# A two-layer attention kernel: ten groups' outputs sent by transfer and divided on GpSimd, and the sums sent ahead of the operands

## The reference

```python
# first block
xn = x * rsqrt(mean(x * x) + EPS) * rms_w
scale, shift = split(cond @ w_cond)
q, k, v = split((xn * (1 + scale) + shift) @ w_qkv)
q, k = rope(q), rope(k)
attn = softmax(einsum("bqhd,bkhd->bhqk", q, k) * DH ** -0.5)
x = einsum("bhqk,bkhd->bqhd", attn, v) @ w_out + x
# second block
xn = layer_norm(x, norm_w, norm_b)
q, k, v = xn @ q_w + q_b, xn @ k_w + k_b, (xn @ v_w + v_b) * mask
att = softmax(q k^T + (1 - mask) * -1e6)
y = att @ v
e = silu(cond) @ emb_w + emb_b
h = layer_norm(y, sb_norm_w, sb_norm_b) * (1 + scale_of(e)) + shift_of(e)
x = x + silu(h) @ out_w + out_b
```

## Time and profile before

| | us |
|---|---|
| median of 3 runs | 491.29 (490.81 to 492.58) |
| profiled execution | 491.88 |
| its span (first to last instruction) | 489.7 |
| PE busy | 478.3 (98%) |
| DVE busy | 385.4 (79%) |
| ACT busy | 342.3 (70%) |
| POOL busy | 313.6 (64%) |

### The profile page before, as it was taken

How to read it: one execution, slowest core, us unless ns; L and a number is a source line. 1 busy time by engine, 2 the same in 40 slices (tenths; PEclk the granted TensorE clock), 3 DMA queues, 4 the chain that set the end, 5 groups by cost and what they waited for, 6 DMA issues and landing times.

```text
span 489.7 us, 9703 instructions
## 1 busy us (share of the span) xinstructions
PE 478.3 (98%) x3197; PEld 179.7 (37%) x3197; DVE 385.4 (79%) x989; ACT 342.3 (70%) x677; POOL 313.6 (64%) x445
## 2 busy tenths in 40 slices
PE   7999899999999999999999999999999999999996
PEld 3553322322443325332443235334333323333234
DVE  3767896999886796859776698867899999999124
ACT  2662567898667785968667785776787788777853
POOL 5569976899885996789646792859990055005501
PEclk9999999999999999999999999999999999999999
DMA  7775156355322465225502361114311121111011
GB/s 255 200 199 190 48 170 228 112 154 157 117 66 68 126 172 152 62 80 139 151 13 69 110 182 46 46 39 116 108 46 44 45 88 45 44 46 45 1 44 44
DMA packets 41577, 49.79 MB, mean 102 GB/s; under 512 B 12388, under 2 KB 34036, under 8 KB 41272
## 3 DMA queue, kind: packets, MB, share of 16 engines
q1 hardware_dynamic: 33336, 31.84, 22.2%
q0 software_dynamic: 7904, 16.03, 11.3%
q10 hardware_dynamic: 288, 1.31, 0.8%
HBM read 27.62 MB, written 19.01 MB: 95 GB/s over the span
## 4 chain that ended last, share of the span: by engine, by line
PE 74%; DVE 12%; POOL 5%; issue 3%; DMA 2%; ACT 1%; SPq 0%; DVEq 0%; POOLq 0%; ACTq 0%
PE bank L596 18%; PE bank L642 11%; PE bank L570 10%; PE bank L579 10%; PE bank L558 9%; DVE masked L955 7%; PE bank L653 6%; PE bank L670 5%; DVE row_max L958 2%; PE bank L627 2%; POOL XN L930 1%; DMA sums<-oT 1%; PE bank L611 1%; ACT probs L780 1%; PE bank L604 1%
## 5 line engine op out<-in xcount | busy, mean ns | idle before, releaser
L780 ACT ACTIVATE probs<-bank 128x512 f32<-128x512 f32 x512 | 269.3, 600 | 71.7 <-PE bank L570 70.9
L958 DVE TENSOR_REDUCE row_max<-bank 128x1 f32<-128x512 f32 x256 | 159.4, 681 | 34.0 <-PE bank L579 33.7
L579 PE MATMUL bank<-k_s,q_s 64*128 64x512 f16 x512 | 178.7, 382 | 2.3 <-DVE row_max L958 1.2
L955 DVE CUSTOM_DVE_ANT_0 masked<-bank,mask_bias 128x512 bf16<-128x512 f32 x256 | 161.7, 686 | 19.2 <-PE bank L579 18.7
L558 PE MATMUL bank<-q_s,k_s 64*128 64x512 f16 x512 | 151.4, 380 | 0.3
L570 PE MATMUL bank<-shift,kx 64*128 64x512 f16 x512 | 148.7, 376 | 0.4 <-DMA shift<-shift_rows 0.4
L596 PE MATMUL bank<-probs,v_aug 128*17 128x512 f32 x1024 | 135.5, 598 | 0.7 <-ACT probs L780 0.7
L579 PEld LDWEIGHTS bank<-k_s,q_s 64*128 64x128 f16 x512 | 46.2, 93 | 157.1 <-DVE row_max L958 70.9
L642 PE MATMUL bank<-xT,wqkv 128*128 128x512 f32 x128 | 59.6, 606 | 1.0 <-DVE xT L1096 0.6
L570 PEld LDWEIGHTS bank<-shift,kx 64*128 64x128 f16 x512 | 46.8, 95 | 34.1 <-DMA shift<-shift_rows 0.9
L1236 POOL TENSOR_SCALAR scaled<-row_max 128x16 f32<-128x16 f32 x30 | 7.7, 255 | 79.9 <-DVE row_max L955 44.5
(11 more groups left out here) (123 smaller groups left out, 478.9 us busy)
## 6 DMA issues: line engine op xcount, KB each, us to landing
q_s<-q_parts SPq DMA_DIRECT2D x32, 256.0 KB, 3.2
k_s<-k_parts SPq DMA_DIRECT2D x32, 256.0 KB, 4.1
k_parts<-parts POOLq DMA_DIRECT2D x62, 128.0 KB, 3.1
q_parts<-parts POOLq DMA_DIRECT2D x60, 128.0 KB, 3.0
X<-in_x SPq DMA_DIRECT2D x4, 512.0 KB, 7.3
O<-oT SPq DMA_DIRECT2D x64, 32.0 KB, 2.0
roped<-inverses SPq DMA_DIRECT2D x16, 128.0 KB
y<-X SPq DMA_DIRECT2D x7, 256.0 KB, 2.2
```

The costliest lines, as they stand in the source:

```text
L579: nc.tensor.matmul(bank, m.q_s[slot][rows, i, queries], m.k_s[slot][rows, i, :], start=True, stop=True).then_inc(q.d_made, 1)
L780: act.activation(m.probs[k][:, h, :], bank, ACT.Exp, scale=1.0 if s >= B * NG else float(DH) ** -0.5)\
L955: dve.tensor_tensor_reduce(m.masked[D["max", n, k, h] % ND][:, :], bank, m.mask_bias[:, b, :], 1.0, LOWEST, ALU.add, ALU.max, to)\
L958: dve.tensor_reduce(to, bank, AX.X, ALU.max).then_inc(q.d_done, 1)
```

## The change

Groups 16 to 25 (`SENT` = 26) leave `turn_output` and `write_output` and go the first layer's way: sums, inverses and output rows by transfer. Their sums are inverted on Pool, as a power with exponent -1 on 128 partitions by 16 columns, and Pool divides the chunk in place. Then PE turns the chunk back (`turn_back`, four transposes for two groups) and ACT copies it to `tokens`, which lies where a weight was. Groups 26 to 31 stay with the transposes. Turns, `y` and statistics of the second layer move to other steps, Pool's list is written anew, and SP sends the sums ahead of the operands; the tile for the sums is doubled.

```diff
+SENT = LAYER + NG * (B - 2) + NG // 2
...
-PIECES[20] = ((), qk(1, LAST, 2, 3), (), v(1, LAST))
-PIECES[22] = (*one(turn("f1", 0)), (), ())
-PIECES[23] = ((), (), y(1, 0)[:1], ())
-PIECES[24] = ((), (), (), y(1, 0)[1:])
-PIECES[26] = (*one(turn("f1", 1)), (), ())
-PIECES[27] = ((), (), y(1, 1)[:1], ())
-PIECES[28] = ((), (), (), y(1, 1)[1:])
+PIECES[20] = ((), qk(1, LAST, 2, 3) + (("back", 0, 0),), (), ())
+PIECES[21] = ((), (), (("back", 0, 1),), v(1, LAST))
+PIECES[23] = (*one(turn("f1", 0)), (), (("back", 1, 0),))
+PIECES[24] = ((), (), y(1, 0)[:1], ())
+PIECES[25] = ((), (), (("back", 1, 1),), y(1, 0)[1:])
+PIECES[27] = (*one(turn("f1", 1)), (), (("back", 2, 0),))
+PIECES[28] = ((), (), y(1, 1)[:1], y(1, 1)[1:])
...
-for _b in range(B - 1):
-    STATISTICS[20 + NG * _b, 3] = ("f1", _b)
+for _b, _s in enumerate((21, 25, 28)):
+    STATISTICS[_s, 3] = ("f1", _b)
...
-        if op == "output" and k == 2 and s > LAYER:
+        if op == "output" and k == 2 and s > SENT:
             yield op, s - 1
-        if op == "output" and k == 3 and 0 < s <= LAYER:
+        if op == "output" and k == 3 and 0 < s <= SENT:
             yield "sums", s - 1
...
+        m.tokens = [m.wc[:, 2 * i:2 * i + 2, :].rearrange("p k n -> p (k n)").rearrange("p (t c) -> p t c", c=C)
+                    for i in range(2)]
...
-        m.sums = sb("sums", [P, KT * G])
+        m.sums = [sb(f"sums{i}", [P, KT * G]) for i in range(2)]
...
+    def turn_back(piece):
+        _, b, c = piece
+        bank = a_free(A[piece])
+        pe.wait_ge(q.divided, normalised(B + b, c))
+        for t in range(TPB):
+            last = nc.tensor.transpose(bank[:, t * P:(t + 1) * P], m.raw[b % 2][:, c, t * P:(t + 1) * P], m.ident[:, :])
+        last.then_inc(q.a_made, 1)
...
-        if s > LAYER:
+        if s > SENT:
             act.wait_ge(q.d_made, D["output", s - 1] + 1)
         elif s:
             act.wait_ge(q.output_out, group_out(s - 1))
...
+    def back(piece):
+        _, b, c = piece
+        bank = made(A[piece])
+        if b >= 2:
+            act.wait_ge(q.xn_made, TPB * NORMAL.index(("f1", b - 2)))
+        act.activation(m.tokens[b % 2][:, :, c * P:(c + 1) * P], bank.rearrange("p (t n) -> p t n", n=P), ACT.Copy)\
+            .then_inc(q.a_done, 1)
...
-        if op == "sums":
+        if op == "sums" and at[0] < LAYER:
             invert(*at)
...
-    def divide(b, c):
-        use = USES.index(("f0", b))
-        pool.wait_ge(q.output_out, group_out(NG * b + 2 * c + 1))
-        pool.wait_ge(q.inv_in[c], 32 * (b + 1))
-        await_read(pool, q, use - 2)
-        pool.tensor_tensor(m.xT[use % 2][:, c, :], m.raw[b % 2][:, c, :], m.inverse[c][:, :], ALU.mult)\
-            .then_inc(q.divided, 1)
+    def divide(pu, c):
+        layer, b = divmod(pu, B)
+        pool.wait_ge(q.output_out, group_out(NG * pu + 2 * c + 1))
+        pool.wait_ge(q.inv_in[c], 32 * (pu + 1))
+        to = raw = m.raw[b % 2][:, c, :]
+        if layer == 0:
+            use = USES.index(("f0", b))
+            await_read(pool, q, use - 2)
+            to = m.xT[use % 2][:, c, :]
+        pool.tensor_tensor(to, raw, m.inverse[c][:, :], ALU.mult).then_inc(q.divided, 1)
+    def invert(s):
+        pool.wait_ge(q.sums_in, 16 * (s + 1))
+        pool.wait_ge(q.inv_out, 16 * s)
+        pool.tensor_tensor(m.inv_sum[:, :, :, :].rearrange("p t h w -> p (t h w)"), m.sums[s % 2][:, :], m.minus_one[:, :],
+                           ALU.pow).then_inc(q.inv_made, 1)
...
-    for b in range(LAST):
-        negate(NG * (B + b) + 6)
-        rstd("f1", b)
-        normal("f1", b)
-        if b == 0:
-            add_bias(LAST, 0)
-        negate(NG * (B + b) + 7)
-        if b == 0:
-            add_bias(LAST, 1)
+    def silu(b):
         for h in range(CT):
             i, h = silu_ready(pool, q, ("turn", "f1", b, h))
             pool.tensor_scalar(m.tanh[h], m.tanh[h], 1.0, None, ALU.add).then_inc(q.tanh_step, 1)
             pool.wait_ge(q.tanh_step, CT * b + h + 1)
             pool.tensor_tensor(m.xT[i][:, h, :], m.tanh[h], m.halved[h], ALU.mult).then_inc(q.silu_made, 1)
-        for n in (NG * (B + b) + 8, NG * (B + b) + 9):
-            if n in POOL_SHIFTS:
-                negate(n)
+    pool.wait_ge(q.one_made, 1)
+    invert(16)
+    invert(17)
+    normalise(LAST)
+    divide(B, 0)
+    add_output_bias(LAST)
+    add_bias(LAST - 1, 0)
+    invert(18)
+    add_bias(LAST - 1, 1)
+    negate(21)
+    split(B + LAST, 0)
+    split(B + LAST, 1)
+    invert(19)
+    negate(22)
+    divide(B, 1)
+    invert(20)
+    split(B + LAST, 2)
+    split(B + LAST, 3)
+    negate(23)
+    rstd("f1", 0)
+    normal("f1", 0)
+    invert(21)
+    negate(24)
+    divide(B + 1, 0)
+    silu(0)
+    negate(25)
+    invert(22)
+    invert(23)
+    add_bias(LAST, 0)
+    negate(26)
+    divide(B + 1, 1)
+    invert(24)
+    add_bias(LAST, 1)
+    negate(27)
+    rstd("f1", 1)
+    normal("f1", 1)
+    invert(25)
+    negate(28)
+    divide(B + 2, 0)
+    silu(1)
+    negate(29)
+    negate(GROUPS - 2)
+    rstd("f1", 2)
+    normal("f1", 2)
+    negate(GROUPS - 1)
+    silu(2)
...
-        if s:
-            sp.wait_ge(q.inv_made, s)
-        sp.dma_start(m.sums[:, :], m.oT[DH::W32, :].rearrange("h (c n) -> h c n", n=KT * G)).then_inc(q.sums_in, 16)
+        if s >= 2:
+            sp.wait_ge(q.inv_made, s - 1)
+        sp.dma_start(m.sums[s % 2][:, :], m.oT[DH::W32, :].rearrange("h (c n) -> h c n", n=KT * G)).then_inc(q.sums_in, 16)
...
-        if b >= 2:
+        if b >= B + 2:
+            sp.wait_ge(q.a_made, A["back", b - 2 - B, g // 2] + 1)
+        elif b >= 2:
             sp.wait_ge(q.divided, normalised(b - 2, g // 2))
...
+        if 1 < s <= LAYER + 1:
+            inverses_in(s - 2)
+        if 0 < s <= SENT:
+            sums(s - 1)
         if 0 < s and exists(s + 3):
             operands(s + 3)
-        if 0 < s <= LAYER:
-            sums(s - 1)
         if exists(s + 1):
             shift(s + 1)
-        if 0 < s <= LAYER:
+        if 0 < s <= SENT:
             raw_output(s - 1)
         if s == 0:
             operands(s + 3)
-        if 0 < s <= LAYER:
+        if 0 < s <= SENT:
             inverses_out(s - 1)
+        if LAYER < s <= SENT:
             inverses_in(s - 1)
```

More of the change, by code:

```diff
@@ L161 @@
 HIGH_BEHIND = [("qk", 0, 0, 2), ("qk", 0, 0, 3), ("turn", "p0", 1, 1), ("v", 0, 0, 1)]
-OUT_AT = {25: 0, 29: 1, 32: 2}
+OUT_AT = {26: 0, 29: 1, 32: 2}
 USES = [("p0", 0), ("p0", 1), ("p0", 2), ("p0", 3), ("f0", 0), ("p1", 0), ("f0", 1), ("p1", 1), ("f0", 2), ("p1", 2),
@@ L278, in chunk_rows, with normalised @@
     return slice(G * DH * (g % 2), G * DH * (g % 2 + 1))
-def normalised(b, c):
-    return CT * b + c + 1
+def normalised(pu, c):
+    return CT * pu + c + 1
 def await_shift(engine, q, n):
@@ L384, in build @@
         m.minus_half = sb("minus_half", [P, NT])
+        m.minus_one = sb("minus_one", [P, KT * G])
         m.stats = sb("stats", [P, NT, 6])
@@ L430, in build @@
         q.inv_made = sem("inv_made")
+        q.one_made = sem("one_made")
         q.xn_made = sem("xn_made")
@@ L752, in tensor @@
                 turn_tokens(piece)
+            if piece[0] == "back":
+                turn_back(piece)
             if piece[0] == "qk":
@@ L909, in scalar @@
                 tokens(piece)
+            if piece[0] == "back":
+                back(piece)
             if piece[0] == "qk":
@@ L974, in invert @@
             dve.wait_ge(q.inv_out, 16 * s)
-        dve.reciprocal(m.inv_sum[:, :, :, :].rearrange("p t h w -> p (t h w)"), m.sums[:, :]).then_inc(q.inv_made, 1)
+        dve.reciprocal(m.inv_sum[:, :, :, :].rearrange("p t h w -> p (t h w)"), m.sums[s % 2][:, :]).then_inc(q.inv_made, 1)
     def write_output(s):
@@ L979, in write_output @@
         bank = made(D["output", s]).rearrange("p (t h w) -> p t h w", t=KT, h=G)
[L980 to L984, removed]
+        if s == SENT:
+            dve.wait_ge(q.inv_out, 16 * SENT)
+        if s == SENT or g == 0:
             dve.wait_ge(q.xn_made, TPB * NORMAL.index(("f1", pu - 2 - B)))
-        if s > LAYER:
+        if s > SENT:
             dve.wait_ge(q.d_done, D["output", s - 1] + 1)
@@ L1018, in take_statistics @@
         else:
-            dve.wait_ge(q.d_done, D["output", NG * (B + b) + NG - 1] + 1)
-            statistics(kind, b, lambda t: m.O[b % 2][:, t, :])
+            dve.wait_ge(q.a_done, max(A[piece] for piece in A if piece[:2] == ("back", b)) + 1)
+            if NG * (B + b) + NG > SENT:
+                dve.wait_ge(q.d_done, D["output", NG * (B + b) + NG - 1] + 1)
+            statistics(kind, b, lambda t: m.tokens[b % 2][:, t, :])
         aggregate(kind, b)
@@ L1113, in last_batch @@
     def last_batch():
-        O = m.O[LAST % 2]
+        O = m.tokens[LAST % 2]
         steps = [TPB]
@@ L1180, in vector @@
                 for t in range(TPB):
-                    dve.bn_stats(m.last_stats[:, t, 0, :], m.O[LAST % 2][:, t, 0:EARLY]).then_inc(q.last_step, 1)
```

(21 more changed lines are left out.)

4 lines of the change are left out of this document (2 added, 2 removed).

## The result

The changed kernel took **495.91 us** (median; 494.51 to 498.32), the kernel before on the same chip 491.60 (490.81 to 494.16): ratio 1.0101, 95% interval 1.0083 to 1.0120 (the medians alone give 1.0088). It is slower by about 1%; the medians differ by 4.3 us, and 492.0 was forecast.

The account below looks back on a forecast made before the run. PE paced some second-layer windows and DVE others, so savings had to come from both. Work removed and added -4.2, SP order -1.3 and waits for Pool +6.2 gave +0.7, so 492.0 us against the 491.29 median; range 486 to 498.

Parts of the forecast that it names:

- the forecast's own: Main outcome: PE waits for Pool's queue as predicted, time 489.5 to 495 us; chance 0.50.
- Removed and added on PE and DVE: Second layer, windows 17 to 28, nothing late: transposes and output work leave, turns back come; -4.2 us.
- 22 and 23: Windows 22 and 23: 10.7 (DVE, one halving) and 10.85 (PE, turn and turn back), 21.6 for 23.1, -1.5 us.
- The order on SP: First layer: sums ahead of operands on SP remove DVE's wait for sums in one window; -1.3 us.
- Pool's inversions: Each power on 16 columns takes 3.05 us on Pool, extrapolated from 2 and 4 columns; bounds 1.04 and 4.2.
- The waits: Second layer: three PE waits hanging on Pool's in-order queue together add 6.2 us.
- First: Step 21, turn back (0,1): PE waits 1.9 us for Pool's divide.
- Second: Step 23, turn back (1,0): PE waits 1.35 us for Pool's divide.
- Third: Shift of group 26: PE waits 3.4 us behind Pool's chain and SP's wait for inversion 22; 2.9 counted.
- Pool keeps up: Rival: inversions of 2.0 us or less remove most waits; 485.8 us without any wait; chance 0.27.
- Pool becomes the bound: Rival: slower inversions in the three chains decide from 3.3 us each; 501.2 us at 4.2 each; chance 0.18.
- The exchange hurts: Rival: operands behind the sums on SP come late in the first layer; about 498 us, or 495; chance 0.05.

Follow-up runs that it names:

- run 5: Changed kernel with a multiply of the same shapes replacing Pool's power, so the second layer's ten sums are not inverted: 488.51 us, ratio 0.9949 to the kernel before.
- run 1: Kernel before with only the SP exchange: sums ahead of operands, two tiles for the sums, inverses' broadcast read next round: 490.75 us, ratio 1.0003.
- Run 10: Kernel before, unchanged, profiled in a second execution: window 13 lasted 9.97 us, windows 17 to 28 lasted 157.07.
- run 11: Changed kernel with eight matmuls on zeros put on PE ahead of its wait for the shift of group 25: 496.78 us, ratio 1.0120 to the kernel before.
- run 6: Changed kernel with inversion 22 moved up on Pool and the silu split into halves around negation 25: 492.74 us, ratio 1.0047 to the kernel before.
- run 7: Changed kernel with silu split around negation 25, inversion 22 moved up, and last batch's output bias moved behind negation of group 30: 491.15 us, ratio 1.0003.
- run 2: Changed kernel with inversion 22 moved up on Pool, ahead of the silu of batch 0 and negation 25: 495.92 us, ratio 1.0110 to the kernel before.
- run 3: Changed kernel with the shift ahead of the operand loads on SP in the second layer: 500.46 us, ratio 1.0215 to the kernel before.
- run 4: Changed kernel with all ten second-layer inversions on DVE instead of Pool: 490.97 us, ratio 1.0006 to the kernel before.
- run 8: Changed kernel with second-layer inversions on DVE, taken in key tile 2 instead of 3, and last batch's output bias moved later on Pool: 489.07 us, ratio 0.9972.

## Why the prediction was right in its mechanism and 3.9 us short

The 495.91 lie inside the range of 486 to 498, which covers most of the rivals too, but above the forecast's own 489.5 to 495; and the likeliest outcome named was a difference within 0.5% (0.39), not a slower kernel (0.34). Lengths in us, from copy to copy:

| windows | before | forecast, nothing late | run 5 | changed |
|---|---|---|---|---|
| 17 | 10.58 | 9.95 | 9.97 | 9.97 |
| 18, 19 | 32.79 | 31.9 | 31.91 | 32.09 |
| 20, 21 | 29.81 | 28.1 | 28.35 | 30.05 |
| 22, 23 | 23.14 | 21.6 | 22.09 | 22.09 |
| 24, 25 | 24.78 | 24.8 | 24.72 | 29.37 |
| 26 to 28 | 35.98 | 36.5 | 37.32 | 37.33 |
| sum | 157.09 | 152.9 | 154.36 | 160.90 |

*Removed and added on PE and DVE: -4.2 forecast, -2.7 in run 5.* The first two rows hold to 0.02: an output's transposes are worth what the earlier trace rows said. Of the 1.5 that are missing, 0.5 lie in windows 22 and 23 and 0.8 in 26 to 28. The step that failed is "22 and 23: 10.7 (DVE: one halving, 0.8) and 10.85 (PE: a turn and a turn back)"; they lasted 11.33 and 10.76. The timelines of DVE and of ACT in the changed kernel:

```profile
367.12 0.81 DVE L1136 TENSOR_SCALAR tables<-bank,mod 128x512 f32<-128x512 f32 x1
...
370.29 0.81 DVE L1136 TENSOR_SCALAR tables<-bank,mod 128x512 f32<-128x512 f32 x1
...
378.02 0.69 DVE L984 CUSTOM_DVE_ANT_0 masked<-bank,mask_bias 128x512 bf16<-128x512 f32 x1 [0.43 <-PE bank L588]
```
```profile
367.96 0.63 ACT L829 ACTIVATE tables<-tables 128x512 f32<-128x512 f32 x1 [0.76 <-DVE tables L1136]
...
369.45 0.60 ACT L809 ACTIVATE oT<-bank 128x512 f32<-128x512 f32 x1
```

From 355.93 until it waits 0.43 for PE ahead of 378.02, 22.09 in all, DVE has no idle time that the rows show, and both halvings stand in its queue there; the sum made DVE the longer side for one of them only. The copy that ends window 22, at 369.45, comes before the second halving. But ACT had waited 0.76 for the first and took its tanh ahead, so that this copy began 0.8 after PE's last values; the copy before it had followed at once. These are readings of the rows; no run moves a halving. Window 26 is built alike and also lasted 11.33, and 28 takes both halves of y; "+0.5" for 26 to 28 measured 1.3.

*The order on SP: -1.3 forecast, nothing in run 1.* One wait in one execution was read as a property of the order. Run 10 shows the old order with 0.3 of it and a window of 9.97.

*Pool's inversions: 3.05 forecast, 2.92.* The extrapolation over columns from the earlier trace rows held: twelve columns more than 1044 ns for four are 0.157 each. A multiply of the same shape took 0.22, so it is the power that is dear. Against DVE's reciprocal at 0.245 it is a factor of 12. The Trainium skill's factor of about two (GPSIMD Engine Reference, section 3, Performance versus the Vector engine) doesn't reach this operation.

*The waits: +6.2 forecast, +6.5 as changed kernel less run 5.* That the three together come so near the forecast is luck, as the sizes shifted among them:
- First, 1.9 forecast: windows 18 to 21 differ by 1.87. Here too errors cancelled: the sums of group 17 landed 3.3 after their issue (2.0 put), but the divide read the broadcast 3.8 after its issue (4.5 put).
- Second, 1.35 forecast: none. Pool took 27.9 from divide to divide (29.0 forecast), mostly because the broadcast was again read 3.8 after its issue; PE, with both halvings ahead of it, came 28.35 after the first divide (27.65 forecast). The margin of 1.35 was less than the errors of both sides.
- Third, 2.9 forecast: windows 24 and 25 differ by 4.65. Pool's chain from the end of divide (1,0) at 374.78 to the end of negation 26 at 397.61 took 22.8 instead of 21.4. All its pieces measured as put to 0.2 but one, the landing of the sums: 3.58 instead of 2.0. "Come late inside it", said of the shift of 25, is borne out twice. In the changed kernel PE turned the shift of 26 at 397.75, 0.14 after its negation's end and without a wait: the wait for 25 and the slow clock had used up the time for which it would have stood there. And with the wait for 25 filled, in run 11, the wait for 26 appears and the sum of the windows doesn't fall (30.12, against 29.37).

In sum -2.7 and +6.5 for -4.2, -1.3 and +6.2: +3.8 instead of +0.7. The medians differ by 4.3; the last 0.5 isn't explained by the profile, which is of the shortest of the six executions.

*The rivals.* "Pool keeps up" has its condition tested by run 5: at 0.22 an inversion the time is 488.5, not 485.8, since the gain was put too high. "Pool becomes the bound" asked for 3.3 or more and fell with the 2.92; runs 6 and 7 show that it was the order; Pool was busy only 113.8 of 160.9. "The exchange hurts" fell with run 1. So the loss is the forecast's own mechanism. Of the 3.1 us by which the sum was short, 2.8 are gain that did not come (1.5 in the windows, 1.3 on SP) and 0.3 are waits.

## What to carry to other kernels

When work moves to an engine with a queue in order, write its queue down as one chain through every engine that is blocked by it: here Pool's inversion held SP, SP held the next sums, and those held Pool. Filling one wait or moving one step forward (runs 2, 3 and 11) only moved the wait elsewhere; taking work out of the chain (runs 4, 5 and 7), or an order that pushes neither the inversion nor the negation back (run 6), brought time back. And look at a second execution before booking the removal of a wait that stands once in one trace.

## What the runs showed of the hardware

- The landing of a small transfer depends on what left just before. In the changed kernel's second layer the 8 KB of sums land, by the last increment of their semaphore, 1.9 to 2.0 after issue in three rounds where the 128 KB broadcast of the inverses had left over 2.5 before on the same queue (issues at 313.89, 328.69 and 410.21), 2.6 after it where it had left 2.3 before (396.93), and 3.0 to 4.3 after it in the five where it had left 0.7 to 0.9 before (from 286.64 to 386.65). It isn't the broadcast alone: at 358.75, 7.4 behind one, it took 2.9; Pool had been issuing transfers of parts until 358.21. The Trainium skill (DMA: Bandwidth & Descriptors, Queues, rings and completion order) says that a transfer's semaphore increment lands only after the earlier writes of the same DMA engine; the five rounds agree with that. The forecast's sum should have had 3.5 for this landing.
- The granted clock fell from 1.00 to 0.50 after PE had idled for 2.2 (changed kernel, at 392.4), 3.2 (run 2), 2.0 (run 4) and 2.1 (run 8), but not after 2.0 in run 5 (at 239.75), 2.2 in run 3 (at 344.26) or 2.1 in run 11 (at 346.9). With the clock kept up, window 24 was 1.25 shorter (run 11), though nothing was won in the end. The rows give no limit between the waits that cost clock and those that don't.
